# Gated experts of a recurrent block: routing weights brought to the experts' rows by transfers in place of a tenth product, and a second accumulator

## Time and profile before

| | us |
|---|---|
| median of 3 runs | 3836.93 |
| lowest and highest | 3836.32, 3841.73 |
| the profiled execution's own time | 3835.93 |
| its span, first to last instruction | 3834.3 |
| routing, from its first DVE step on the scores to the store's issue | 1512.4 to 1554.8 |
| experts: first transfer to the first up product | 1559.9 to 1582.0 |
| experts: loop, to the start of the last copy out | 1582.0 to 1897.5 |

### The profile page before, as it was taken

The page is one execution under the profiler, slowest core; times in us unless marked ns, Lnnn a source line. Parts: engine busy times, 40 slices in busy tenths (PEclk is TensorE's granted clock), DMA queues, the critical chain, the costliest instruction groups (busy, mean ns, idle before and its releaser), DMA issues. The chain is left out here.

```text
span 3834.3 us, 64458 instructions
## 1 busy us (share of the span) xinstructions
PE 2977.1 (78%) x20107; PEld 1311.3 (34%) x20108; DVE 2419.3 (63%) x3442; ACT 1841.6 (48%) x2929; POOL 1435.8 (37%) x984
## 2 busy tenths in 40 slices
PE   3999999999999966699825999999669420838983
PEld 1333333333333326333321222222246320525661
DVE  5666666666666623788867899999543459334532
ACT  2555555555555520344533888889524430443331
POOL 0887787787787740100000010101036307520000
PEclk9999999999999987899956999999879755969955
DMA  2011111111111123200014222222111202130012
GB/s 78 28 43 50 38 43 50 38 43 50 38 43 50 38 94 122 52 1 0 1 54 108 56 47 55 55 48 55 50 51 45 65 30 92 47 93 16 8 38 66
DMA packets 264326, 189.82 MB, mean 50 GB/s; under 512 B 146165, under 2 KB 208494, under 8 KB 263400
## 3 DMA queue, kind: packets, MB, share of 16 engines
q1 hardware_dynamic: 255720, 172.58, 16.0%
q0 software_dynamic: 8512, 16.11, 1.3%
HBM read 102.26 MB, written 66.44 MB: 44 GB/s over the span
## 5 line engine op out<-in xcount | busy, mean ns | idle before, releaser
L312 POOL TENSOR_TENSOR attn_esum<-attn_esum,attn_prob 128x1024 f32<-128x1024 f32 x384 | 904.5, 2355 | 126.1 <-ACT attn_prob L463 105.2
L523 DVE TENSOR_REDUCE attn_half_max<-attn_peek 128x2 f32<-128x1024 f32 x512 | 627.0, 1225 | 439.0 <-PE attn_peek L350 439.0
L463 ACT ACTIVATE attn_prob<-attn_score 128x1024 f32<-128x1024 f32 x512 | 512.4, 1021 | 331.5 <-PE attn_score L333 330.8
L842 DVE TENSOR_REDUCE attn_half_max<-attn_peek 128x2 f32<-128x1024 f32 x512 | 588.1, 1218 | 51.4 <-PE attn_peek L761 51.2
L825 ACT ACTIVATE attn_prob<-attn_score 128x512 f32<-128x512 f32 x1024 | 556.1, 596 | 111.7 <-PE attn_score L775 99.1
L381 PE MATMUL attn_acc<-attn_prob,attn_v 128*64 128x512 f32 x2048 | 496.2, 605 | 0.1
L791 PE MATMUL attn_acc<-attn_prob,attn_v 128*32 128x256 f32 x4096 | 338.9, 404 | 9.1 <-ACT attn_out L817 7.6
L1616 POOL DMA_INDIRECT sorted_x<-attn_sent_rows,attn_send x64 | 62.5, 977 | 599.8 <-PE attn_score L775 564.3
L761 PE MATMUL attn_peek<-attn_ke,attn_qe 48*128 48x512 bf16 x1024 | 208.7, 404 | 44.2 <-DMA attn_ke<-k 32.0
L775 PE MATMUL attn_score<-attn_qe,attn_ke 49*128 49x512 bf16 x1024 | 206.7, 400 | 37.1 <-DMA attn_qe<-max 29.9
L350 PE MATMUL attn_peek<-attn_hi 64*128 64x512 f16 x1024 | 200.0, 387 | 44.8 <-DVE attn_half_max L523 44.8
(11 more groups left out here) (453 smaller groups left out, 4603.3 us busy)
## 6 DMA issues: line engine op xcount, KB each, us to landing
attn_xb<-attn_x_all SPq DMA_DIRECT2D x66, 256.0 KB, 2.5
attn_invB<-inv SPq DMA_DIRECT2D x64, 256.0 KB, 4.0
o<-attn_out SPq DMA_DIRECT2D x32, 512.0 KB, 2.6
out_o<-o SPq DMA_DIRECT2D x8, 2048.0 KB, 8.9
mix_f<-picked SPq DMA_DIRECT2D x16, 512.0 KB, 7.1
experts_x<-sorted_x SPq DMA_DIRECT2D x112, 65.0 KB
attn_qe<-q SPq DMA_DIRECT2D x192, 32.0 KB
attn_ke<-k SPq DMA_DIRECT2D x192, 32.0 KB
```

Of the source, the lines that this page charges most:

```text
L312: nc.gpsimd.tensor_tensor(own, before, prob[:, u % NPROB, :, :], ALU.add).then_inc(added, 1)
L463: nc.scalar.activation(prob[:, u % NPROB, :, :], score[:, u % 2, :, :], ACT.Exp).then_inc(exped, 1)
L523: V.tensor_reduce(half_max[:, half, :, t], peek[:], AX.X, ALU.max, negate=True).then_inc(maxed, 1)
L842: V.tensor_reduce(half_max[:, half, PAIR * pair:PAIR * (pair + 1), t], peek[:, m % NPEEK, :, :], AX.X, ALU.max, negate=True).then_inc(maxe ...
```

## The change

Routing no longer splits `comb` into three parts: PE turns the f32 values (32 transposes, 32x128), and `cT` in HBM is [32, 4096] f32. In the experts' stage `cT` in SBUF, the table `sel`, POOL's program and the tenth product are gone. In their place SP issues a transfer for each of the steps 0 to 15 of each chunk: it writes `share` [128, 512] of one of 8 ring buffers, with row 2k of `cT` on partitions 0 to 63 and row 2k+1 on partitions 64 to 127. The load for a buffer waits until the h that last read it is done (`mixed`), and h waits for the load (`share_in`). The accumulator is doubled: chunks alternate between two, and the wait on `copied` is for the chunk before last.

```diff
@@ grouped_routing_stage
-        cT = st.sb("cT", [PARTS * E, TOK], BF16)
+        cT = st.sb("cT", [E, TOK])
-        trb = st.ps("trb", [PARTS * E, 2, 8, P], BF16)
+        trb = st.ps("trb", [E, 2, 8, P])
...
-                last = nc.tensor.transpose(trb[:, t // 8 % 2, t % 8, :], parts[:, t, :, :].rearrange("p a e -> p (a e)"), ident16[:])
+                last = nc.tensor.transpose(trb[:, t // 8 % 2, t % 8, :], comb[:, t, :], ident[:])
...
-            link(V.tensor_tensor(comb[:], pick[:], per_tok(red), ALU.mult))
-            link(V.tensor_copy(parts[:, :, 0, :], comb[:]))
-            link(V.tensor_tensor(rest[:], comb[:], parts[:, :, 0, :], ALU.subtract))
-            link(V.tensor_copy(parts[:, :, 1, :], rest[:]))
-            link(V.tensor_tensor(rest[:], rest[:], parts[:, :, 1, :], ALU.subtract))
-            V.tensor_copy(parts[:, :, 2, :], rest[:]).then_inc(parts_ready, 1)
+            V.tensor_tensor(comb[:], pick[:], per_tok(red), ALU.mult).then_inc(comb_ready, 1)
@@ gated_experts_stage
+    RING = 8
+    HALF = P // 2
-        cT = st.sb("cT", [96, TOK], BF16)
-        sel = st.sb("sel", [96, NSEL * P], BF16)
+        share = st.sb("share", [P, RING, CH])
-        rep = st.ps("rep", [P, 2, CH])
-        acc = st.ps("acc", [P, CH])
+        acc = st.ps("acc", [P, 2, CH])
...
         @block.sync
         def _(sp):
-            sp.dma_start(cT[:], cT_d[:, :]).then_inc(c_loaded, DMA)
...
-        @block.gpsimd
-        def _(pool):
-            width = P // 2
-            nc.gpsimd.memset(sel[:], 1.0).then_inc(made, 1)
...
+            def load_shares(i, slot, first):
+
+                for k in range(NSEL):
+                    if not (first and k < RING):
+                        sp.wait_ge(mixed, i * HT + (k - RING + 1 if k >= RING else k - RING))
+                    sp.dma_start(share[:, k % RING, :],
+                                 cT_d[2 * k:2 * k + 2, bass.ds(i * CH, CH)].unsqueeze(1).to_broadcast([2, HALF, CH])).then_inc(share_in[k % RING], DMA)
+
+            iterations(sp, load_shares)
...
             def down(i, slot, k):
                 pe.wait_ge(h_split, i * HT + k + 1)
-                if k == 0 and not (isinstance(i, int) and i == 0):
-                    pe.wait_ge(copied, i)
-                product(acc[:], down_w, slice(k * D, (k + 1) * D), h_parts, (slice(None), (slot * HT + k) % 2, slice(None)),
+                if k == 0 and not (isinstance(i, int) and i < 2):
+                    pe.wait_ge(copied, i - 1)
+                product(acc[:, slot, :], down_w, slice(k * D, (k + 1) * D), h_parts, (slice(None), (slot * HT + k) % 2, slice(None)),
...
-                    ins = product(up[1][:, s, :], up_w[1], own, x_parts, (slice(None), tok), True, True)
-                    if k < NSEL:
-                        ins = nc.tensor.matmul(rep[:, s, :], sel[:, own], cT[:, tok], start=True, stop=True)
-                    ins.then_inc(second_up, 1)
+                    product(up[1][:, s, :], up_w[1], own, x_parts, (slice(None), tok), True, True).then_inc(second_up, 1)
...
                     if k < NSEL:
                         V.tensor_tensor(g[:, s, :], up[1][:, s, :], a[:, s, :], ALU.mult).then_inc(tmp_ready, 1)
+                        dve.wait_ge(share_in[k % RING], DMA * (2 * i + k // RING + 1))
                         dve.wait_ge(tmp_ready, i * NSEL + k + 1)
-                    V.scalar_tensor_tensor(out=h[:, s, :], in0=(rep if k < NSEL else up[1])[:, s, :], scalar=H_SCALE / UP,
+                    V.scalar_tensor_tensor(out=h[:, s, :], in0=share[:, k % RING, :] if k < NSEL else up[1][:, s, :], scalar=H_SCALE / UP,
                                            in1=(g if k < NSEL else a)[:, s, :], op0=ALU.mult, op1=ALU.mult).then_inc(mixed, 1)
@@ recurrent_block_kernel
-    cT = scratch("cT", [96, TOK], BF16)
+    cT = scratch("cT", [32, TOK])
```

More of the change, by code:

```diff
@@ L1193, in grouped_routing_stage @@
     E = 32
-    PARTS = 3
     with Stage(nc, "route0") as st:
@@ L1199, in grouped_routing_stage @@
         comb = st.sb("comb", [P, NT, E])
-        rest = st.sb("rest", [P, NT, E])
-        parts = st.sb("parts", [P, NT, PARTS, E], BF16)
-        ident16 = st.sb("ident16", [P, P], BF16)
         best = st.sb("best", [P, NT, 8])
@@ L1208, in grouped_routing_stage @@
         red = st.sb("red", [P, NT])
-        cT = st.sb("cT", [PARTS * E, TOK], BF16)
+        cT = st.sb("cT", [E, TOK])
         lg = st.ps("lg", [P, NT, E])
         wt = st.ps("wt", [P, E])
-        trb = st.ps("trb", [PARTS * E, 2, 8, P], BF16)
+        trb = st.ps("trb", [E, 2, 8, P])
         consts, made, stored = (st.sem(n) for n in ("consts", "made", "stored"))
-        w_turned, w_ready, logits, dve_step, act_out, parts_ready, b_turned, b_copied = (
-            st.sem(n) for n in ("w_turned", "w_ready", "logits", "dve_step", "act_out", "parts_ready", "b_turned", "b_copied"))
+        w_turned, w_ready, logits, dve_step, act_out, comb_ready, b_turned, b_copied = (
+            st.sem(n) for n in ("w_turned", "w_ready", "logits", "dve_step", "act_out", "comb_ready", "b_turned", "b_copied"))
         block = st.block()
@@ L1229, in _ @@
             nc.gpsimd.memset(before[:], 1.0).then_inc(made, 1)
-            nc.gpsimd.tensor_copy(ident16[:], ident[:]).then_inc(made, 1)
-            pool.wait_ge(made, 2)
+            pool.wait_ge(made, 1)
             nc.gpsimd.affine_select(out=before[:], in_=before[:], compare_op=ALU.is_ge, fill=0.0, base=-1,
@@ L1243, in _ @@
             last.then_inc(logits, 1)
-            pe.wait_ge(made, 3)
-            pe.wait_ge(parts_ready, 1)
+            pe.wait_ge(comb_ready, 1)
             for t in range(NT):
@@ L1279, in _ @@
             dve.wait_ge(consts, NCONST * DMA)
-            dve.wait_ge(made, 3)
+            dve.wait_ge(made, 2)
             bias_f = bias_b[:].unsqueeze(1).to_broadcast(full)
@@ L1348, in gated_experts_stage @@
         up = [st.ps(f"up{n}", [P, 2, CH]) for n in range(2)]
-        rep = st.ps("rep", [P, 2, CH])
-        acc = st.ps("acc", [P, CH])
-        c_loaded, made, acted, tmp_ready, mixed, h_high, h_split, summed, copied = (
-            st.sem(n) for n in ("c_loaded", "made", "acted", "tmp_ready", "mixed", "h_high", "h_split", "summed", "copied"))
+        acc = st.ps("acc", [P, 2, CH])
+        acted, tmp_ready, mixed, h_high, h_split, summed, copied = (
+            st.sem(n) for n in ("acted", "tmp_ready", "mixed", "h_high", "h_split", "summed", "copied"))
         first_up, second_up, w_turned, w_high, w_split, x_high, x_split = (
             st.sem(n) for n in ("first_up", "second_up", "w_turned", "w_high", "w_split", "x_high", "x_split"))
-        consts = [st.sem(f"consts{n}") for n in range(3)]
+        consts, share_in = [st.sem(f"consts{n}") for n in range(3)], [st.sem(f"share_in{n}") for n in range(RING)]
         block = st.block()
@@ L1414, in _ @@
             pe.wait_ge(x_split, NX)
-            pe.wait_ge(made, 7)
-            pe.wait_ge(c_loaded, DMA)
             def product(out, ws, cols, xs, own, start, stop):
@@ L1473, in high, with copy_out @@
                 nc.scalar.activation(h_parts[0][:, s, :], h[:, s, :], ACT.Copy).then_inc(h_high, 1)
-            def copy_out(i):
+            def copy_out(i, slot):
                 act.wait_ge(summed, (i + 1) * HT)
-                nc.scalar.activation(fT[:, bass.ds(i * CH, CH)], acc[:], ACT.Copy, scale=1.0 / (H_SCALE * W_SCALE)).then_inc(copied, 1)
+                nc.scalar.activation(fT[:, bass.ds(i * CH, CH)], acc[:, slot, :], ACT.Copy, scale=1.0 / (H_SCALE * W_SCALE)).then_inc(copied, 1)
             def body(i, slot, first):
@@ L1490, in body @@
                     if k == 2 and not first:
-                        copy_out(i - 1)
+                        copy_out(i - 1, 1 - slot)
             iterations(act, body)
             high(NCH - 1, 1, HT - 1, True)
-            copy_out(NCH - 1)
+            copy_out(NCH - 1, 1)
         @block.vector
```

## The result

The changed kernel takes 4187.24 us (median of 4 runs, 4180.73 to 4195.13) beside 3838.32 for the kernel before (4 runs on the same chip): ratio 1.0909, 95% interval [1.0888, 1.093]. Slower, as forecast, and inside the range; 28 us under the forecast of 4215. The profiled execution took 4189.2 us.

The account below looks back on a forecast made before the run. A ring of PE and DVE waits bounds the experts' loop, 4.50 us per two steps. Loads: 1574 + 696 = 2270, plus 5 is 2275 against 1897.5, +378 with savings inside; 3836.93 + 378 = 4215 us, range 4125 to 4567.

Parts of the forecast that it names:

- The load uses two engines: Experts' loop: each share load goes to 2 of 16 DMA engines, 5.44 us a load; chance 0.89.
- The price of a packet: Share loads in the experts' loop: 0.085 us per 2 KB packet, 64 packets on each engine, 5.44 us a load.
- the two clean rows: Trace prices per 2 KB packet: 0.090 us from HBM reads, 0.081 from a store of 4 KB packets halved.
- When the loads begin: Share loads start when the expert weight transfers leave the engines: about 1577 us before, 1574 after.
- The tail: From the last share through h, low, shared step and last down product to the final copy: another 5 us.
- The rest of the kernel: Everything behind the experts' loop, including the narrow attention: no change in the forecast.
- Routing, net zero give or take 1.5: Routing: five DVE passes save 4.8 us; f32 transposes take 7.9 in place of 3.8, copies 0.5 more.
- the row of mix0-3: Trace basis for routing's f32 transposes: 96 took 23.6 us, 0.246 each, so 7.9 for 32.
- First up product 3 us sooner by the load of cT: Ahead of the loop: without the 768 KB load, 3.0 us, expert weights and first up product come 3 us sooner.
- rival (a): All 16 engines take each share load: 1.02 us, hidden; sum -21 us, 3816 in total; chance 0.11.
- -12 and -6: Experts' loop savings: 12 us from dropping the tenth product, 6 us from two accumulators at 7 chunk boundaries.
- The 0.128 of the broadcasts at 155 us: Rival (two engines, dear packets): share-load packets cost 0.128 us as in broadcasts rereading rows; 8.2 us a load, +730, 4567.

Follow-up runs that it names:

- the halves: Changed kernel with each share load issued as two transfers, one source row to 64 partitions each: 3876.25 us, ratio 0.998 to the kernel before.
- with four engines: Changed kernel with routing weights stored twice and each load reading four source rows, 32 partitions each: 3908.33 us, ratio 1.0056 to the kernel before.
- with eight: Changed kernel with four stores of the routing weights and each load reading eight source rows, 16 partitions each: 3827.57 us, ratio 0.9982 to the kernel before.

## Why the prediction was right, point by point

- *The load uses two engines.* Right: two closing packets a load, 51 GB/s (forecast 48), share 0.13 (0.12), h idle 3.04 us (about 3), the clock down from 1.00 to 0.83. The question the trace before left open, what unequal sides give (2 source, 128 destination), is settled for a source with the smaller count: 2, 4 and 8 engines for 2, 4 and 8 source rows beside 128 partitions, and 16 for 64 and 64. A destination with the smaller count was not tried. The rule of the Trainium skill, DMA: Bandwidth & Descriptors, section "Why a DMA increments its semaphore by 16 and not by 1", gives just these numbers.
- *The price of a packet*, "I take 0.085, between the two clean rows". 0.081 measured: the end of the earlier trace rows, the store of 4 KB packets halved, was right, and the step was 5.18 us, not 5.44. 128 x 0.26 = 33 us too much, the largest term of the error. The figure of that page of the Trainium skill, about 27 GiB/s an engine, would have given 4.5 us; two engines moved 51 GB/s, 23.6 GiB/s each.
- *When the loads begin*, "1574 after". The last share is used at 2233.4; 128 x 5.18 = 663 before that is 1570.6, 3.4 earlier. That is when the weights leave the engines: the DMA share falls in the microsecond from 1570 to 1571, and before the change in that from 1577 to 1578, so they left 7 us sooner where I had put 3. Until then the share loads, issued from 1568.1 on, hardly ran: from 1568 to 1570 us one packet of 468 is as large as 2 KB. The tail, put at 5, was 4.5. The stretches (columns of the earlier trace rows), after and then before:

```profile
1569.00:1570.00 1.00, 0.10 (x1) 0.00 (x0) 1.00 (x3) 0.84 (x3) 0.00 (x0) 1.00 1.02 186
1570.00:1571.00 1.00, 0.16 (x1) 0.17 (x2) 0.77 (x2) 0.00 (x0) 0.00 (x0) 1.00 0.20 57
...
1576.00:1577.00 1.00, 0.34 (x2) 0.14 (x1) 1.00 (x2) 0.98 (x3) 0.39 (x1) 1.00 0.90 168
1577.00:1578.00 1.00, 0.04 (x1) 0.04 (x1) 0.95 (x3) 0.00 (x0) 0.00 (x0) 1.00 0.10 26
```

- *The rest of the kernel*, put at nothing: +12.9. The sum then closes: 4214 (the forecast against the profiled execution) - 33 - 3.4 - 0.5 + 12.9 = 4190, and it took 4189.2. The total came within 28 us by some luck: the packets were 33 us cheaper than forecast, and an attention stage that the prediction had put at nothing gave 13 of it back.
- *Routing, net zero give or take 1.5.* From the start of `comb` to the issue of its store 10.6 us before (1544.16 to 1554.77), 8.65 after (1541.85 to 1550.50), so 2.0 less, just outside the band. The transposes took 5.95 us, where the row of mix0-3 had made me put 7.9; the copies are 1.21 each in f32 where the bf16 ones took 0.69, but three of four stand beside transposes.
- *First up product 3 us sooner by the load of cT.* From the stage's start to that product 22.1 us before and 19.6 after, 2.5 sooner. But more than the load went: the four low parts of x on DVE took 1.22 us each where the median had been 2.90 beside POOL's work on the table, which I had put at nothing. Those two causes were not separated. The product itself came 7.1 us earlier, at 1574.90: 2.5 are these, 2.0 the routing's, 0.3 lie between its store and the weights' issue, and 2.3 were there already at the routing's first DVE step (1510.1, before 1512.4), ahead of anything that the change touches. The sooner weights did reach the end, since they let the loads begin sooner; the sooner product did not, as the loads end to end were the bound.
- *The gains of rival (a),* -12 and -6. Right in sum, 18.0, seen in the halves; the parts are some 10 (by subtraction) and 7.7.

## What to carry to other kernels

Ask of every transfer how many engines it can use, and read it off the closing packets of transfers of the same form: in the runs here the smaller of the two outermost counts, up to 16, decided (where they differed it was the source's), and a two there left a load of 256 KB at 51 GB/s, whether it read two rows or 128, with eight buffers or four. A broadcast cut into one transfer per source row cost one more issue and brought the step from 5.18 to 2.15 us.

When a stage far behind the edit changes its length, look at the instruction queue before explaining it by data: count its packets in both kernels. Dummy instructions in idle time test it. Here they took 13.8 us off the attention of the kernel with the halves, where the halves themselves had taken 18.0 off the loop.

## What I had not expected of the hardware

- 64 PE instructions more or less, 500 us and more ahead of a hardware loop, made the stage with that loop 13 to 21 us (2 to 3%) longer or shorter, with 53 or 54 packets of 16 KB more or less in the instruction queue; in the longer ones PE's idle time shows 18 to 20 us of "issue".
- SP's own instruction lasts long when the loads ahead of it are slow: the issue of a share load took a median of 4.83 us (562 ns at least), with four engines 2.26, with eight 0.62. That SP is held until the queue has room again is my reading; no run tried it. Its waits on buffers hardly mattered: with 8 or 4 buffers the loop took the same time.
- The price of a 2 KB packet hardly depended on the number of engines. From the DMA share, closing packets counted in, it is 0.083 with two, 0.262 x 16 x 21.6 / 1106 = 0.082 with four, and in the same way 0.088 with eight and 0.085 with sixteen. The 0.128 of the broadcasts at 155 us was not repeated by any load of a row 64 times here.
